# A one-core macaron block: pieces of the first stage split and moved, scales by a TensorE sum, attention's first group begun with its values

## The chip, the cores and the metric

One Trainium2 chip, one core of it. The metric is the time of one execution on the device in microseconds (us); for the kernel before it is the median of three runs.

## The reference, cut to what matters

x has 2 sequences of 2048 tokens of 1024 values. Three layers follow one another, each on a layer norm of x:

```python
x = x + 0.5 * ffn(layernorm(x))
x = x + attn(layernorm(x), w_attn, w_o)   # blocks of 128 tokens, each sees itself and the one before
x = x + 0.5 * ffn(layernorm(x))
# ffn(x): thought = layer_norm(x)[:, -1, :] @ agg_w + agg_b       (one row for each sequence)
#         4 times: thought += gelu(layer_norm(thought) @ d1_w + d1_b) @ d2_w + d2_b
#         gate = sigmoid(x @ gate_w + gate_b)
#         return layer_norm(x + gate * (thought @ bc_w + bc_b))
# attn:   weights = square(relu(masked q k^T)); out = (weights @ v) @ w_o^T, no softmax
```

All values are float32. The thought is a chain over one row for each sequence, with 4 x 2 large weight matrices of 16 MB; everything else works on 32 tiles of 128 tokens.

## The kernel before, in words

**One written plan.** `whole_plan` makes a list of pieces such as `("gate", n, h, third)` or `("norm", n)`. The programs of TensorE, ScalarE, DVE, GpSimd and SyncE (which issues all transfers) each walk the same list and issue their own part of every piece, in its order, with semaphore waits in front. An engine that waits holds up all that stands behind it in its own program, and nothing else. `paced(main, other, pace)` puts `pace` pieces of the second list behind each piece of the first that TensorE works on (`PE_PIECES`); `("rest",)` is an empty piece, for distance. `with_thought` spreads the steps of the thought chain (`t_...`) by an estimate of TensorE's time.

**Stages.** Stage 1 folds w_q and w_k into one matrix (`fold`, "qk"), then turns w_o and folds it with w_v ("vo"), and makes the gates of the 32 tiles (`gate`, two halves of three thirds of 8 matmuls each, 1.7 to 1.9 us a third). In this stage the thought of the first ffn runs beside them: its weights (512 KB a load) stream through a ring of slots, read from HBM twice or three times; in its first round ScalarE takes sums of their magnitudes (L1381), later it rounds them to a first float16 part and DVE makes the second (`t_high`, `t_low`, L1400 and L1754), which SyncE stores. Stage 2 is attention by groups of two tiles: q by 8 pieces, v, scores, collect; beside it the first ffn's end for the next group (`prep_...`). Stage 3 is the second ffn.

**Float16 pairs.** Weights and tokens are split in two float16 parts each, and a product is three float16 products. A weight matrix is scaled first by a power of two from its largest magnitude: `gate_max` or the fold's own maxima for each of 8 row blocks (L1463, L1470), `scale_a`, where DVE takes their maximum in each partition (L1475) and GpSimd the maximum over partitions (L1844), and `scale_b`, five small DVE steps. Then ScalarE rounds (`round`, L1266) and DVE takes the rest (`split`, L1496).

**A gate tile.** SyncE fetches x (`x`, L873) into a ring of 3; DVE takes moments and GpSimd the reciprocal root (L1423 to L1433, L1818, L1825); ScalarE applies the norm in the same piece (`norm`, L1282); TensorE turns the tile into two turn banks (`turn`, L1032; w_o goes through the same two banks, `wo_turn`), ScalarE and DVE empty them (L1236, L1274, L1440). The product goes to one of 4 product banks; DVE scales it and adds the bias (L1448), ScalarE takes the sigmoid in the same piece (L1295) and `gate_store` writes it (L877). The split gate weights are themselves written to HBM for stage 3 (`gate_save`, L882), eight transfers of 512 KB during the fold "vo", with the loads of gamma and beta (`params`, L884) behind them.

**The fold.** A finished row block is copied by ScalarE (L1252) into one of 2 slots, whose maximum DVE takes (L1470) and which SyncE stores (`fold_store`, L852); a copy waits until the store of the block two before has landed. The stored blocks come back later by `fold_rows` (L865).

**Attention's first group.** q needs the turned pairs of both of its tiles (`group_turn`, a transposing transfer, L944), v of a tile only that tile's. `plan_products` puts all of q first.

## Time and profile before

| | us |
|---|---|
| median of 3 runs | 2115.19 (2111.64 to 2117.34) |
| the profiled execution, its own time | 2117.86 |
| its span | 2116.6 |
| TensorE busy | 2037.7 (96%) |
| DVE busy | 1173.0 (55%) |
| ScalarE busy | 664.7 (31%) |
| GpSimd busy | 159.0 (8%) |
| mean transfer rate | 263 GB/s |

The profiler took one execution. Busy time is that of instructions; a matmul's end is modelled, so busy TensorE need not be at its peak. In timelines each line is the start, the time taken (both us), the engine, the line of the kernel, the operation and its tiles, the count, and in brackets the idle time before it with what ended it. PE is TensorE, ACT ScalarE, POOL GpSimd, SPq SyncE's queue of issues.

### The profile page before, as it was taken

The page shows a single profiled execution, that of the slowest core. Times are in us where ns is not written, and L with a number is a line of the kernel's source. Part 1 is how long each engine was busy: PE and PEld are TensorE (multiplying, and loading weights), DVE is VectorE, ACT ScalarE, POOL GpSimd, SP SyncE. Part 2 cuts the span into 40 slices and gives each one's busy share as a digit, 9 for nine tenths or more (in the row PEclk, how much of TensorE's full clock was granted, in tenths as well). Part 3 has the DMA queues.
Part 4 walks back from the last instruction along what each step waited for, and adds up shares of the span by engine and source line. Part 5 has one row for each costly group of instructions (what it writes and reads, how often), then busy time and mean ns, then how long its engine had stood idle before and what let it go on. Part 6 is the DMA issues. An engine that isn't in the chain of part 4 may idle for free.

```text
span 2116.6 us, 30247 instructions
## 1 busy us (share of the span) xinstructions
PE 2037.7 (96%) x11872; PEld 1037.0 (49%) x11872; DVE 1173.0 (55%) x2108; ACT 664.7 (31%) x931; POOL 159.0 (8%) x281
## 2 busy tenths in 40 slices
PE   8988989999999999998999999999999999999997
PEld 3333433444333446655665555665556564444443
DVE  2321323554344465567676755655555545888887
ACT  0557322433223232222333221211212113444443
POOL 0000000000000010000000000000000000111111
PEclk9999999999999999999999999999999999999999
DMA  8788897988988833348989799898987947555552
GB/s 340 237 311 341 285 353 269 379 319 320 354 338 333 332 132 118 100 140 299 323 294 327 273 320 293 297 347 283 313 290 278 357 149 221 149 151 154 154 149 80
DMA packets 275213, 555.76 MB, mean 263 GB/s; under 512 B 149040, under 2 KB 149248, under 8 KB 274688
## 3 DMA queue, kind: packets, MB, share of 16 engines
q1 hardware_dynamic: 275072, 553.83, 75.5%
q8 instruction: 95, 1.56, 0.3%
q14 instruction: 46, 0.38, 0.0%
HBM read 406.93 MB, written 113.26 MB: 246 GB/s over the span
## 4 chain that ended last, share of the span: by engine, by line
PE 47%; DMA 3%; DVE 2%; SPq 2%; ACT 1%; issue 1%; POOL 0%; ACTq 0%; DVEq 0%
PE product_banks L1023 41%; PE product_banks L1143 3%; PE thought_acc L1208 3%; DMA thought_units<-parts_scratch 1%; DMA gate_arena<-arena 1%; DMA arena<-in_x 0%; SPq L810 0%; DVE thought_units L1754 0%; SPq L944 0%; DMA thought_units<-in_d_w 0%; ACT arena L1315 0%; PE thought_turn L1216 0%; ACT arena L1318 0%; PE thought_acc L1198 0%; DVE arena L1566 0%
## 5 line engine op out<-in xcount | busy, mean ns | idle before, releaser
L1023 PE MATMUL product_banks<-gate_arena,arena 128*128 128x512 f16 x1536 | 354.1, 382 | 0.0
L1023 PE MATMUL product_banks<-wide_a,thought_units 128*128 128x512 f16 x1536 | 331.7, 379 | 0.0
L1023 PE MATMUL product_banks<-gate_arena,wide_a 128*128 128x256 f16 x2688 | 307.5, 274 | 2.4 <-DMA gate_arena<-arena 2.4
L1023 PE MATMUL product_banks<-wide_b,gate_arena 128*128 128x512 f16 x1344 | 301.8, 380 | 0.0
L1023 PEld LDWEIGHTS product_banks<-gate_arena,wide_a 128*128 128x128 f16 x2688 | 260.4, 98 | 59.5 <-issue 28.9
L1054 PE MATMUL product_banks<-wide_a,wide_b 128*128 128x512 f32 x512 | 240.9, 616 | 7.1 <-DMA wide_a<-in_w_attn 6.3
L1023 PEld LDWEIGHTS product_banks<-gate_arena,arena 128*128 128x128 f16 x1536 | 145.0, 98 | 203.6 <-issue 51.0
L1023 PEld LDWEIGHTS product_banks<-wide_a,thought_units 128*128 128x128 f16 x1536 | 150.3, 98 | 181.6 <-DVE arena L1606 0.5
L1023 PEld LDWEIGHTS product_banks<-wide_b,gate_arena 128*128 128x128 f16 x1344 | 127.2, 98 | 167.5 <-issue 24.9
L1423 DVE BATCH_NORM_STATS2 bn_parts<-arena 128x6 f32<-128x512 f32 x256 | 164.3, 684 | 4.4
L1054 PEld LDWEIGHTS product_banks<-wide_a,wide_b 128*128 128x128 f32 x512 | 95.1, 195 | 137.9 <-issue 137.8
L1448 DVE SCALAR_TENSOR_TENSOR arena<-product_banks,inverse_gate,arena 128x512 f32<-128x512 f32 x64 | 47.9, 750 | 176.5 <-PE product_banks L1023 175.6
L1818 POOL TENSOR_TENSOR token_stats<-stats,minus_half 128x1 f32<-128x1 f32 x96 | 61.3, 639 | 1083.4 <-DVE stats L1431 909.5
L1575 DVE SCALAR_TENSOR_TENSOR gate_arena<-product_banks,gate_arena 128x256 f16<-128x256 f32 x128 | 54.1, 423 | 152.5 <-ACT gate_arena L1330 150.2
L1336 ACT ACTIVATE arena<-product_banks,inverse_vo 128x512 f32<-128x512 f32 x64 | 44.0, 687 | 243.1 <-PE product_banks L1023 243.1
L1208 PE MATMUL thought_acc<-thought_units,thought_parts 128*6 128x512 f16 x1328 | 101.6, 383 | 19.1 <-DMA thought_units<-parts_scratch 10.2
L1143 PE MATMUL product_banks<-arena,key_weights 128*128 128x512 f32 x248 | 112.9, 600 | 6.1 <-issue 3.2
L1818 POOL TENSOR_TENSOR stats<-stats,minus_half 128x1 f32<-128x1 f32 x64 | 65.2, 1019 | 703.6 <-DVE stats L1431 419.3
L1330 ACT ACTIVATE gate_arena<-product_banks 128x256 f16<-128x256 f32 x128 | 41.4, 379 | 222.9 <-PE product_banks L1023 222.9
L1307 ACT ACTIVATE arena<-arena,token_stats 128x1024 f32<-128x1024 f32 x32 | 39.5, 1235 | 226.6 <-DMA arena<-in_x 226.6
L1364 ACT ACTIVATE arena<-arena 128x512 f32<-128x512 f32 x64 | 40.3, 630 | 175.2 <-DVE arena L1448 175.2
L1566 DVE SCALAR_TENSOR_TENSOR arena<-arena 128x1024 f16<-128x1024 f32 x32 | 39.2, 1225 | 97.2 <-ACT arena L1318 97.1
(168 smaller groups left out, 2090.1 us busy)
## 6 DMA issues: line engine op xcount, KB each, us to landing
thought_units<-parts_scratch SPq DMA_DIRECT2D x268, 512.0 KB, 6.1
thought_units<-in_d_w SPq DMA_DIRECT2D x148, 512.0 KB, 6.7
thought_row<-in_d_w SPq DMA_DIRECT2D x76, 512.0 KB, 7.2
arena<-in_x SPq DMA_DIRECT2D x64, 512.0 KB, 8.8
parts_scratch<-thought_units SPq DMA_DIRECT2D x64, 512.0 KB, 6.2
x_scratch<-arena SPq DMA_DIRECT2D x64, 512.0 KB, 6.8
arena<-x_scratch SPq DMA_DIRECT2D x40, 512.0 KB, 6.0
gate_scratch<-arena SPq DMA_DIRECT2D x32, 512.0 KB, 8.3
```

The lines of the kernel that those rows point to most:

```text
L1023: mm = pe.matmul(bank, left(i, k), right(j, k), start=(n == 0), stop=(n == 3 * KD - 1))
L1054: mm = pe.matmul(bank_ap(key), wide_b[:, e, d * P:(d + 1) * P], wide_a[:, e, h * BANK:(h + 1) * BANK], start=(e == 0), stop=(e == KD - 1))
L1143: mm = pe.matmul(bank_ap(key), weights_of(u)[:, side, :], value_slot(other)[:, h * BANK:(h + 1) * BANK], start=(side == 0), stop=(side == ...
L1208: mm = pe.matmul(thought_acc[at:at + PARTS * B, :], value, unit[:, part, h * BANK:(h + 1) * BANK], start=first and part == 0, stop=last an ...
L1307: act.activation(ph_slots[u % PREP_RING], px_slots[u % PREP_RING], ACT.Identity, bias=st[:, 1:2], scale=st[:, 0:1]).then_inc(h0_made, 1)
L1330: act.activation(queries[:, query_place(n * GROUP + i), 0, e - 1:e + 1, :], made[:, i], ACT.Copy, scale=QUERY_SCALE).then_inc(q_high_made, 1)
L1336: act.activation(value_slot(n * GROUP + i)[:, h * BANK:(h + 1) * BANK], bank_ap(key), ACT.Copy, scale=inverse["vo"][:, :]).then_inc(out_of ...
L1364: act.activation(res, res, ACT.Sigmoid).then_inc(gated_3, 1)
L1423: dve.bn_stats(bn_parts[:, h, :], source[:, h * BANK:(h + 1) * BANK]).then_inc(own.up(), 1)
L1448: dve.scalar_tensor_tensor(out=res[:, cols], in0=bank_ap(key), scalar=inverse["gate"][:, :], in1=bias[:, cols], op0=ALU.mult, op1=ALU.add) ...
L1575: low = dve.scalar_tensor_tensor(out=q[:, 1], in0=made[:, i], scalar=QUERY_SCALE, in1=q[:, 0], op0=ALU.mult, op1=ALU.subtract)
L1818: return pool.tensor_tensor(to, st[:, 2:3], minus_half[:, 0:1], ALU.pow)
```

## The change

In stage 1 the sigmoid becomes a piece of its own: that of a tile's first half after the first third of the second half, that of the second half after the first third of the next tile. ScalarE's part of a norm becomes `norm_h`, after the second third of a gate tile (and, for tiles 0 and 1, earlier in the first fold, with DVE's part of norm 1 moved ahead of the turns of tile 0). The pace of the pieces beside the first fold goes from 0.8 to 0.9. For scales DVE's maximum is `scale_t`; in `scale_a` TensorE multiplies it by a matrix filled with 1/1024, which gives every partition the sum over partitions, and DVE scales it back; GpSimd's reduction goes. The scale so comes from a sum of 128 maxima instead of the largest. `scale_a` takes a turn bank. `gate_save` and `params` move from the fold "vo" to the gate tiles behind it, among the row fetches and splits, whose pace goes from 0.3 to 0.6 of a list that is longer by them. In group 0 of attention the six thirds of v of tile 0 come ahead of q. SyncE's, TensorE's and DVE's waits follow the new places.

```diff
@@ -365,8 +365,14 @@
             out.append(("gate", n, h, third))
-            if n and (h, third) == (1, 0):
-                out.append(("gate_store", n - 1))
+            if n and (h, third) == (0, 0):
+                out.append(("sigmoid", n - 1, 1))
+            if (h, third) == (0, 1) and n + 2 < TILES:
+                out.append(("norm_h", n + 2))
+            if (h, third) == (1, 0):
+                out.append(("sigmoid", n, 0))
+                if n:
+                    out.append(("gate_store", n - 1))
     return out
@@ -440,6 +446,10 @@
             products = products[:-PARTS]
+        if n == 0:
+            own = [p for p in products if p[0] == "v" and p[2] == 0]
+            products = own + [p for p in products if p not in own]
         if more:
@@ -489,12 +499,12 @@
     gate_rows += [("gate_max", k) for k in range(KD)]
-    gate_rows += [("scale_a", "gate"), ("rest",), ("rest",), ("scale_b", "gate")]
+    gate_rows += [("scale_t", "gate"), ("rest",), ("scale_a", "gate"), ("rest",), ("scale_b", "gate")]
     gate_rows += rounded_ahead("gate", [])
...
     gate_rows += [("x", 1), ("x", 2)] + [("wo_rows", n) for n in range(wo_ahead)] + [("norm", 0), ("rest",)]
-    gate_rows += [("rest",), ("rest",), ("turn", 0, 0), ("turn", 0, 1), ("norm", 1)]
-    fold_qk = paced(plan_fold("qk"), gate_rows, 0.8, PE_PIECES)
+    gate_rows += [("norm_h", 0), ("norm", 1), ("rest",), ("norm_h", 1), ("turn", 0, 0), ("turn", 0, 1)]
+    fold_qk = paced(plan_fold("qk"), gate_rows, 0.9, PE_PIECES)
     fold_qk.append(("fold_store", "qk", KD - 1))
@@ -502,15 +512,17 @@
     early = paced([p for n in range(EARLY) for p in plan_gate(n)], wo, 0.9, PE_PIECES)
-    save = [("gate_save", k) for k in range(KD)] + [("params",)] + [("rest",)] * 6 + [("half_params",)]
-    fold_vo = paced(plan_fold("vo"), save, 0.5, PE_PIECES)
-    fold_vo.append(("fold_store", "vo", KD - 1))
+    fold_vo = plan_fold("vo") + [("fold_store", "vo", KD - 1)]
     splits = []
     for m in ("qk", "vo"):
-        splits += [("fold_rows", m, 0), ("fold_rows", m, 1), ("scale_a", m), ("rest",), ("scale_b", m)]
+        splits += [("fold_rows", m, 0), ("fold_rows", m, 1), ("scale_t", m), ("rest",), ("scale_a", m), ("rest",), ("scale_b", m)]
         splits += rounded_ahead(m, [("fold_rows", m, k) for k in range(2, KD)])
+    save = [("params",)] + [("rest",)] * 5 + [("half_params",)]
+    for k in range(KD):
+        save += [("gate_save", k)] + [("rest",)] * 3
+    splits = paced(splits, save, 0.75)
     splits += [("prep_fetch", 0), ("rest",), ("rest",), ("prep_norm", 0), ("prep_beta", 0)]
-    gates = paced([p for n in range(EARLY, TILES - LATE) for p in plan_gate(n)], splits, 0.3, PE_PIECES)
+    gates = paced([p for n in range(EARLY, TILES - LATE) for p in plan_gate(n)], splits, 0.6, PE_PIECES)
     out = [("start",)]
@@ -518,7 +530,7 @@
     out += paced([p for n in range(TILES - LATE, TILES) for p in plan_gate(n)], prep, 1.15, PE_PIECES)
-    out.append(("gate_store", TILES - 1))
+    out += [("sigmoid", TILES - 1, 1), ("gate_store", TILES - 1)]
     out.append(("score_scale",))
@@ -553,12 +565,16 @@
 TURN_AT = {piece: n for n, piece in enumerate(
-    p for p in PLAN if p[0] in ("turn", "wo_turn"))}
+    p for p in PLAN if p[0] in ("turn", "wo_turn", "scale_a"))}
 SPLIT_TURN_AT = {piece: n for n, piece in enumerate(
...
+SCALE_AT = {piece[1]: n for n, piece in enumerate(p for p in PLAN if p[0] == "scale_b")}
@@ -1055,6 +1071,14 @@
                         mm.then_inc(product_full, 1)
+            elif kind == "scale_a":
+                m, = a
+                at = TURN_AT[(kind, m)]
+                if at >= TURN_BANKS:
+                    pe.wait_ge(turn_out[at % TURN_BANKS], at // TURN_BANKS)
+                pe.wait_ge(top_found, SCALE_AT[m] + 1)
+                pe.matmul(turn_ap((kind, m))[:, 0:1], mean_maker[:, :], scale_stat[m][:, KD:KD + 1], start=True,
+                          stop=True).then_inc(turn_full, 1)
             elif kind == "wo_turn":
@@ -1088,8 +1112,6 @@
                         pe.wait_ge(group_in[i], 16 * (n + 1))
-                    if n == 0:
-                        pe.wait_ge(split_done, split_total("vo"))
                 group, cols = group_of(n), slice(e * P, (e + 1) * P)
@@ -1103,6 +1125,9 @@
                     await_free(pe, key)
+                    if n == i == h == 0:
+                        pe.wait_ge(group_in[0], 16)
+                        pe.wait_ge(split_done, split_total("vo"))
                 group, cols = group_of(n), slice(h * BANK, (h + 1) * BANK)
@@ -1259,7 +1284,7 @@
                 if k == 0:
-                    act.wait_ge(scale_made, ("gate", "qk", "vo").index(m) + 1)
+                    act.wait_ge(scale_made, SCALE_AT[m] + 1)
                     if m != "gate":
@@ -1274,10 +1299,10 @@
                     turn_out[at % TURN_BANKS], 1)
-            elif kind == "norm":
+            elif kind == "norm_h":
                 n, = a
                 xt, st = x_slots[n % X_RING], token_stats[:, TILE_OF[n], :]
-                act.wait_ge(rstd_made, MOMENT_AT[(kind, n)] + 1)
+                act.wait_ge(rstd_made, MOMENT_AT[("norm", n)] + 1)
                 act.wait_ge(x_in[n % X_RING], 16 * (n // X_RING + 1))
@@ -1288,8 +1313,8 @@
                 round_half((kind, n, h), as_pair(pair_slots[n % PAIR_RING])[:, 0])
-            elif kind == "gate" and a[2] == 2:
-                n, h, _ = a
+            elif kind == "sigmoid":
+                n, h = a
                 await_out(act, ("gate", n, h))
@@ -1471,15 +1496,20 @@
+                at = TURN_AT[(kind, m)]
+                dve.wait_ge(turn_full, at + 1)
+                dve.tensor_scalar(scale_stat[m][:, KD:KD + 1], turn_ap((kind, m))[:, 0:1], float(D), TINY, ALU.mult,
+                                  ALU.max).then_inc(turn_out[at % TURN_BANKS], 1)
+            elif kind == "scale_t":
+                m, = a
                 dve.wait_ge(largest[m], KD)
...
                 top, exponent, scale = (scale_stat[m][:, KD + i:KD + i + 1] for i in range(3))
-                dve.wait_ge(top_shared, ("gate", "qk", "vo").index(m) + 1)
-                dve.tensor_scalar(top, exponent, TINY, None, ALU.max).then_inc(own.up(), 1)
-                dve.wait_ge(own.sem, own.n)
+                await_turned(dve, ("scale_a", m))
                 dve.tensor_scalar(exponent.bitcast(I32), top.bitcast(I32), EXPONENT_BITS, None,
@@ -1838,11 +1868,6 @@
                 pool.wait_ge(zeroed, 1)
-            elif kind == "scale_a":
-                m, = a
-                pool.wait_ge(top_found, ("gate", "qk", "vo").index(m) + 1)
-                pool.partition_all_reduce(scale_stat[m][:, KD + 1:KD + 2], scale_stat[m][:, KD:KD + 1], P,
-                                          bass.bass_isa.ReduceOp.max).then_inc(top_shared, 1)
             elif kind == "norm":
```

## Rows read from the trace of the kernel before

**Rows 1.** The page, part 1: busy us, share of the span, instructions.
```profile
PE 2037.7 (96%) x11872; PEld 1037.0 (49%) x11872; DVE 1173.0 (55%) x2108; ACT 664.7 (31%) x931; POOL 159.0 (8%) x281
```

**Rows 2.** Stretches: length, busy PE, PEld, DVE, ACT, POOL, then PEclk, DMA share, GB/s.
```profile
150.10:229.10 79.00, 61.24 (x351) 27.36 (x351) 19.48 (x49) 53.66 (x94) 2.92 (x8) 0.93 0.88 331
229.10:370.00 140.90, 134.56 (x425) 52.12 (x426) 45.53 (x61) 36.33 (x42) 0.71 (x1) 0.96 0.84 297
370.00:730.00 360.00, 349.64 (x2038) 143.70 (x2037) 157.35 (x341) 118.93 (x158) 24.86 (x52) 1.00 0.90 346
...
784.60:812.40 27.80, 23.73 (x194) 20.13 (x194) 11.90 (x20) 3.84 (x8) 0.55 (x1) 0.88 0.39 135
```

**Rows 3.** Timeline, ScalarE and TensorE, 153 to 180 us.
```profile
153.81 1.24 ACT L1282 ACTIVATE arena<-arena,token_stats 128x1024 f32<-128x1024 f32 x1 [1.84 <-POOL token_stats L1825]
155.10 1.97 PE L1032 MATMUL turn_banks<-identity,arena 128*128 128x128 f32 x8 [5.01 <-ACT arena L1282]
156.86 3.15 PE L1023 MATMUL product_banks<-gate_arena,arena 128*128 128x512 f16 x8
...
161.41 1.89 PE L1023 MATMUL product_banks<-gate_arena,arena 128*128 128x512 f16 x8
...
178.07 1.09 PE L1032 MATMUL turn_banks<-identity,arena 128*128 128x128 f32 x8
```

**Rows 4.** Waits of TensorE for transfers, 156.5 to 229.2 us: total, times, longest.
```profile
PE thought_acc L1198 <- DMA thought_units<-in_d_w: 3.3, 4, 1.6
PE turn_banks L1032 <- DMA arena<-in_w_o: 3.0, 1, 3.0
PE thought_acc L1198 <- DMA thought_row<-in_d_w: 2.7, 2, 1.8
```

**Rows 5.** Waits of ScalarE, 156.5 to 229.2 us: total, times, longest.
```profile
ACT arena L1282 <- POOL token_stats L1825: 10.5, 3, 3.6
ACT arena L1295 <- DVE arena L1448: 6.9, 2, 4.1
```

**Rows 6.** Timeline, 257 to 301 us: TensorE, SyncE's store of the fold, ScalarE.
```profile
257.76 0.60 PE L1208 MATMUL thought_acc<-thought_units,thought_parts 128*6 128x512 f16 x8
258.30 3.70 PE L1054 MATMUL product_banks<-wide_a,wide_b 128*128 128x512 f32 x8
...
279.38 1.17 SPq L852 DMA_DIRECT2D vo_scratch<-arena  x2
...
288.48 1.07 ACT L1252 COPY arena<-product_banks 128x512 f32<-128x512 f32 x2 [11.39 <-DMA vo_scratch<-arena]
...
293.92 1.02 PE L1208 MATMUL thought_acc<-thought_units,thought_parts 128*6 128x512 f16 x8 [6.34 <-DVE t_wide L1761]
294.87 5.91 PE L1054 MATMUL product_banks<-wide_a,wide_b 128*128 128x512 f32 x8
```

**Rows 7.** Stores of the gates' weights (landing; issue ns), and one stretch of 10 us.
```profile
gate_pair_scratch<-gate_arena SPq DMA_DIRECT2D x8, 512.0 KB, 8.2
...
L882 SPq DMA_DIRECT2D gate_pair_scratch<-gate_arena x8: 478/844/1638, 233.5 to 282.2; - x8
...
280.00:290.00 10.00, 7.57 (x24) 2.96 (x16) 0.35 (x1) 1.52 (x3) 0.00 (x0) 1.00 1.02 419
```

**Rows 8.** Timeline where attention begins, and 48 like matmuls later.
```profile
784.72 1.63 SPq L944 DMA_TRANSPOSE thought_units<-arena  x1
...
788.69 23.83 PE L1023 MATMUL product_banks<-thought_units,wide_a 128*128 128x256 f16 x192 [4.07 <-DMA thought_units<-arena]
...
1033.70 5.41 PE L1023 MATMUL product_banks<-gate_arena,wide_a 128*128 128x256 f16 x48
```

**Rows 9.** Timeline, GpSimd's reduction for the scale of qk.
```profile
399.90 0.38 POOL L1844 PARTITION_ALL_REDUCE scale_stat_qk<-scale_stat_qk  x1 [6.71 <-issue]
```

**Rows 10.** Gate rows' issues and landing (us), DVE's thought norm, TensorE behind it.
```profile
22.84 10.20 SPq L836 DMA_DIRECT2D arena<-in_gate_w  x8
...
DMA to landing us min/median/max: 14.9/15.3/15.8
...
42.06 0.50 DVE L1696 TENSOR_SCALAR thought<-centred,t_small 128x8 f32<-128x8 f32 x2 [0.90 <-POOL t_small L1861]
...
43.00 0.29 PE L1178 MATMUL thought_turn<-thought,mean_maker 128*128 128x16 f32 x2
```

**Rows 11.** SyncE's own waits, 0 to 800 us: at `gate_store`.
```profile
SPq L877 <- ACT arena L1295: 17.0, 5, 10.5
```

More of the change, by code:

```diff
@@ L620, in macaron_kernel @@
     d1_bias = sbuf("d1_bias", [P, KH])
-    scale_stat = {m: sbuf(f"scale_stat_{m}", [P, KD + 3]) for m in ("gate", "qk", "vo")}
-    inverse = {m: sbuf(f"inverse_{m}", [P, 1]) for m in ("gate", "qk", "vo")}
+    scale_stat = {m: sbuf(f"scale_stat_{m}", [P, KD + 3]) for m in SCALE_AT}
+    inverse = {m: sbuf(f"inverse_{m}", [P, 1]) for m in SCALE_AT}
     score_scale = sbuf("score_scale", [P, 1])
@@ L717, in macaron_kernel @@
     largest = {m: sem(f"largest_{m}") for m in ("gate", "qk", "vo")}
-    top_found, top_shared = sem("top_found"), sem("top_shared")
+    top_found = sem("top_found")
     high_made, split_done = sem("high_made"), sem("split_done")
@@ L1502, in vector_program @@
             elif kind == "score_scale":
-                dve.wait_ge(scale_made, 3)
+                dve.wait_ge(scale_made, len(SCALE_AT))
                 dve.tensor_scalar(score_scale[:, :], inverse["qk"][:, :], 1.0 / (QUERY_SCALE * TOKEN_SCALE * P),
```

## The prediction, made before the change was run

> **What bounds the kernel now.** I read the page first, then a table of stretches, then the waits of TensorE, then the timeline around its longest waits. TensorE is busy in 2037.7 of 2116.6 us [rows 1]: only about 79 us can be won without taking matmuls away. The stretches show where the edit's share of them lies [rows 2]: 17.8 us idle in 150.1 to 229.1 (early gate tiles and the turning of w_o), 6.3 us in 229.1 to 370 (the second fold), 10.4 us in 370 to 730 (gate tiles with weights split), and 4.1 us in 784.6 to 812.4, where attention begins. So four places count, and each has another cause.
>
> First, 5.01 us before 155.10 [rows 3]: TensorE wants to turn tile 1, whose norm ScalarE ends only then, because DVE's moments came late. Second, the remaining 12.7 us up to 229.1: 9.0 us on transfers [rows 4] and 3.7 us, by subtraction, on ScalarE and DVE emptying turn banks. ScalarE is there stopped at the head of its queue, 10.5 us for GpSimd's reciprocal root and 6.9 us for DVE in front of a sigmoid [rows 5], with bank copies and weight maxima (which SyncE's fetches wait for) behind it. Third, 6.34 us before 293.92: ScalarE cannot copy a finished product of the fold, since the slot's store was issued at 279.38 and freed ScalarE only at 288.48; DVE's copy of the sums, which TensorE wants, is queued behind that [rows 6]. Stores of the gates' weights lie among those transfers and take 8.2 us to land [rows 7]. Fourth, 4.07 us before 788.69, the turned copy of the second token tile, issued at 784.72 [rows 8].
>
> Each of these waits is followed by matmuls at a lower granted clock: the stretch 784.6 to 812.4 has a mean of 0.88, between the levels 1.2 and 2.4 GHz [rows 2], and the same eight operations take longer right after a wait [rows 3, 6].
>
> **The change part by part.**
>
> *Norms apart, tile 1 early.* DVE's and GpSimd's part of norm 1 now stands some six fold pieces before turn 1, ScalarE's part (`norm_h`) in between. The wait of 5.01 us goes. With it goes the slow clock: eight turns in 1.97 instead of 1.09 us, eight matmuls in 3.15 instead of 1.89 us [rows 3]. Together 5.01 + 0.88 + 1.26 = 7.2 us. In later tiles `norm_h` comes after two thirds of a gate product, and still four thirds, some 7 us, before the turn that needs it; one norm takes 1.24 us [rows 3], so nobody waits for it.
>
> *Norms and sigmoids, to 229.1.* No instruction is added; those behind them on ScalarE come earlier. Of the 3.7 us on banks I take half, 1.8. Of the 9.0 us on transfers, 3.0 is a row of w_o whose fetch SyncE issues behind fetches that wait for ScalarE; I take half, 1.5. The rest stays, and grows: the stretch moved 331 GB/s for 79 us [rows 2], 26.1 MB, and 10 us at a full share moved 419 GB/s [rows 7], so it can't be shorter than 62.4 us. TensorE without waits would need about 79 - 17.8 - 2.1 = 59. What is won at 155 thus meets transfers that are nearly full; I give 2.0 us back. Net 1.3 us won; bounds: 8 won (the stretch near its 62.4, beyond the 7.2) and 5 lost. The lower clock after the last turns I leave as it is.
>
> *Sigmoids and the queue of SyncE.* The sigmoid of a tile's second half moves behind the next tile's first third, `gate_store` stays. Between them are three thirds, some 5 us, for one short operation. SyncE already waits for sigmoids there, 17.0 us in 5 waits [rows 11], and the fetches behind it wait with it. I cost it at nothing, for the three thirds cover it; without that cover it is the slower rival.
>
> *Gates' weights stored later.* Eight stores of 0.52 MB, issued from 233.5 to 282.2, and two parameter loads leave the second fold; at 419 GB/s each holds the transfer engines 1.25 us, so the eight hold them 10 us, and SyncE for some 0.5 to 1.6 us each [rows 7]. Without them the fetches on which SyncE's earlier steps wait land sooner, and so the fold's store is both issued and landed some us earlier. TensorE stood from 293.92 - 6.34 = 287.6 on, so all of the wait goes if ScalarE's 288.48 comes forward by 6.3 us, and part of it with less. The wait is worth 6.34 + (1.02 - 0.60) + (5.91 - 3.70) = 9.0 us, taking the slow rows against the same forms at full clock [rows 6]; I take 8, as this wait has two causes and both shrink. Bounds: 2 (only the issue order changes) and 9. The parameters are first read long after, by `half_params`, which moves with them.
>
> *The same stores in the gate stretch.* It has 10.4 us of idle TensorE at a transfer share of 0.90, 346 GB/s [rows 2]. The ten transfers add 12.5 us of transfer time to 36 us of room; the rows to be split also come some 20% denser, as 200 pieces shrink to about 165. Where the share is full, a store pushes every fetch behind it back by 1.25 us. I take 3.5 us lost; bounds 0 and 8.
>
> By a page of the Trainium skill, DMA: Bandwidth & Descriptors, section Where 436 GB/s comes from, about 358 GB/s on the HBM side bind such transfers. By it the 124.6 MB of this stretch and 5.2 MB more would need 362.5 us, more than the stretch now lasts, so every added store would cost its full time there. The trace speaks against it, with 419 GB/s over 10 us.
>
> *Scales from a sum by TensorE.* DVE's steps stay as many. Three partition reductions leave GpSimd (0.38 us each, with 6.71 us idle before the second) [rows 9]; no engine was held up by them while TensorE ran, so 0 won. TensorE gains three tiny matmuls, under 0.3 us each by its nearest row [rows 10]: 0.4. It also waits now for DVE's maximum, two plan pieces behind; behind a late maximum all of TensorE would stand. For qk and vo DVE has pieces to spare. For the gates, the maxima of the rows move forward: one more stands in front of DVE's `t_var`, and the first now stands ahead of the fold's own two maxima. The rows land 14.9 us after issue at 22.84, so the first near 37.7 and the second near 39; DVE's step that ended at 42.56 moves back by about one maximum of 1.2 us and the wait for the first row, 1.5 to 2 us, and TensorE's 43.00 has 0.4 us of room [rows 10]. 1.5 us lost, bounds 0 and 3.
>
> *Attention begins with values.* v of tile 0 needs only the first turned copy, so 6 thirds, some 10 us, cover the second. Won: 4.07 and the slow clock, 23.83 us for 192 matmuls against 4 x 5.41 [rows 8] = 2.2; 6.3 us. Late next: the first scores have 3 instead of 9 thirds between them and the last queries, some 5 us in which DVE must finish the last pair of queries behind the tokens it prepares; I expect no wait. Bounds 2 and 6.5.
>
> **Sum.** -7.2 - 1.3 - 8.0 + 3.5 + 0.4 + 1.5 - 6.3 = -17.4 us. The profiled execution took 2117.86 us (span 2116.6, 1.3 around it), 2.7 above the median of 2115.19. 2117.9 - 17.4 = 2100.5 on its own scale, 2115.2 - 17.4 = **2098 us** for a median. Stages after this one only shift.
>
> **The rivals.**
> - *Transfers are the bound* (0.20). The 155 to 229 stretch gives 2 us in all, the fold 6, the gate stretch takes 8, the start of attention gives 6, scales take 2: -4, **2111 us**. For: shares of 0.88 and 0.90 [rows 2]. Against: a tenth of the transfer time is still unused. The page above would have it so.
> - *The fold's wait stays* (0.13): the store is late since SyncE waits for splits of thought weights, not since the bus is full. Then 8 becomes 1, -10.4: **2105 us**. For: SyncE's queue waits for ScalarE and DVE at every such split. Against: that chain itself waits for fetches slowed by the stores.
> - *More comes back* (0.12): the stretch to 229 reaches its bound of 8 instead of 1.3, since ScalarE's 17.4 us of waits [rows 5] were behind most of what TensorE waits for, and the gate stretch takes nothing: -17.4 - 6.7 - 3.5 = -27.6, **2088 us**.
> - *SyncE waits for late sigmoids* (0.06), slower: in each of 25 middle tiles it stands at `gate_store` for a sigmoid now behind turns, and thought fetches behind it come later. It decides once the wait exceeds what the ring of fetched weights covers; at 1 us each 25 us are lost, -17.4 + 25 = +7.6, **2123 us**. Against: 5 waits in 32 stores now.
> - That the edit does not do what it says has no room here: the order of instructions is written out. Little net effect by a mixture of mishaps: 0.04.
>
> **How the numbers follow.** My forecast has 0.45 and spans 2092 to 2104. The range over cases reaches from 2087 to 2111, leaving out half of the best case, part of the transfer case and the slower ones. A measurement of this kernel can tell about 0.3%, 6.3 us, from no change: faster means under 2108.8. Faster: 0.45 + 0.13 + 0.12 and a half of 0.20, 0.80. Same 0.14, slower 0.06.
>
> **What would show it.** Right: no TensorE wait of 5 us near 150 and none near 287, the q product without a wait, stores of the gates' weights spread over 380 to 650, granted clock 1.0 in the 10 us after 150 and after 287. Wrong: idle TensorE in 370 to 730 over 20 us; a wait of ScalarE on the fold's store still near 11 us; SyncE's waits at `gate_store` summing to over 40 us; a new wait before the first scores. I'd be wrong altogether if the time around 229 came out where it is now.

## The result, and the profile after

2105.35 us median against 2114.78 for the kernel before, 11 runs each: ratio 0.996, 95% interval 0.9943 to 0.9976. It is 0.4% faster, 8.5 us by the ratio and 9.4 by the medians, about half of what was forecast. The median lies outside 2092 to 2104, the span given to the forecast alone, and inside 2087 to 2111, the range over all cases. The profiled execution took 2104.01 us, span 2102.8. The page and the same stretches as in [rows 1, 2]:

```profile
PE 2035.0 (97%) x11878; PEld 1034.0 (49%) x11878; DVE 1172.2 (56%) x2108; ACT 664.0 (32%) x931; POOL 161.1 (8%) x278
```

```profile
150.10:229.10 79.00, 72.06 (x387) 29.98 (x386) 20.39 (x46) 56.06 (x97) 2.18 (x6) 0.96 0.90 350
229.10:370.00 140.90, 138.05 (x488) 53.30 (x488) 49.52 (x69) 42.35 (x49) 1.43 (x3) 0.99 0.81 292
370.00:730.00 360.00, 344.35 (x1997) 141.36 (x1995) 155.80 (x344) 113.62 (x151) 27.20 (x50) 0.99 0.90 346
784.60:812.40 27.80, 27.80 (x225) 21.85 (x224) 16.13 (x25) 8.45 (x14) 1.26 (x3) 1.00 0.36 123
```

TensorE's idle time fell from 17.8 to 6.9, from 6.3 to 2.9 and from 4.1 to 0 us in three stretches, and rose from 10.4 to 15.7 in the gate stretch. Fixed windows cut the work at different places in two kernels, so everything below goes by the work: the start of the same matmul in each timeline, in one profiled execution of each kernel. Matmuls 128 to 192 of the first fold take 39.4 in both and are left out. Numbers in us:

| from, to | before | after | difference | forecast |
|---|---|---|---|---|
| span's start, first matmul | 5.9 | 5.5 | -0.4 | |
| first fold, matmuls 0 to 128 | 65.1 | 66.6 | +1.5 | +1.5, gate maxima |
| first fold, 192 to 224 | 22.3 | 24.3 | +2.0 | |
| from there to the second fold | 96.4 | 87.5 | -8.9 | -8.5, tile 1 and the freer ScalarE |
| the second fold | 143.1 | 135.9 | -7.1 | -8.0 |
| gate tiles 3 to 27 | 368.3 | 375.2 | +6.9 | +3.9 |
| gate tile 28 to attention's first collect | 97.9 | 91.6 | -6.3 | -6.3 |
| the rest | 1278.3 | 1276.8 | -1.5 | |

The sum is -13.8, that of the two spans. ScalarE's waits for GpSimd and DVE in 156.5 to 229.2 [rows 5] are gone, and TensorE's for transfers are 5.8 instead of 9.0 [rows 4]. These are ScalarE's three longest there, then TensorE's:

```profile
ACT wide_a L1299 <- PE turn_banks L1048: 11.9, 8, 3.2
ACT thought_units L1406 <- DMA thought_row<-in_d_w: 2.4, 3, 1.7
ACT thought_units L1406 <- DMA thought_units<-in_d_w: 1.4, 2, 1.2
...
PE thought_acc L1223 <- DMA thought_units<-in_d_w: 2.9, 2, 2.1
PE thought_acc L1223 <- DMA thought_row<-in_d_w: 2.9, 1, 2.9
```

The timeline of after, at the places of [rows 10, 3, 6, 8] in turn, with the one new wait of 2 us ahead of the second fold, at 134.79:

```profile
43.20 0.49 DVE L1726 TENSOR_SCALAR thought<-centred,t_small 128x8 f32<-128x8 f32 x2 [0.90 <-POOL t_small L1886]
43.76 0.40 PE L1203 MATMUL thought_turn<-thought,mean_maker 128*128 128x16 f32 x2 [0.88 <-DVE thought L1726]
...
134.79 1.04 PE L1223 MATMUL thought_acc<-thought_units,narrow_in 128*6 128x512 f32 x8 [2.04 <-DMA thought_units<-in_d_w]
...
154.85 1.09 PE L1048 MATMUL turn_banks<-identity,arena 128*128 128x128 f32 x8
155.78 1.89 PE L1039 MATMUL product_banks<-gate_arena,arena 128*128 128x512 f16 x8
...
269.77 1.26 SPq L868 DMA_DIRECT2D vo_scratch<-arena  x2
276.51 1.07 ACT L1277 COPY arena<-product_banks 128x512 f32<-128x512 f32 x2 [8.99 <-DMA vo_scratch<-arena]
281.95 0.60 PE L1233 MATMUL thought_acc<-thought_units,thought_parts 128*6 128x512 f16 x8 [2.85 <-DVE t_wide L1791]
...
778.28 10.52 PE L1039 MATMUL product_banks<-wide_b,thought_units 128*128 128x512 f16 x48
788.64 21.12 PE L1039 MATMUL product_banks<-thought_units,wide_a 128*128 128x256 f16 x192
...
825.99 0.67 PE L1168 MATMUL product_banks<-arena,key_weights 128*128 128x512 f32 x1 [1.91 <-DVE key_weights L1623]
```

TensorE turns tile 1 with no wait and at full clock (1.09 us instead of 1.97). Behind the wait at 134.79 the granted clock was 0.83 on average from 136 to 146, and what that costs falls into the fourth difference of the table, not into the third. ScalarE still waits 8.99 us for the fold's store, and TensorE 2.85 of the 6.34 us. Attention begins without a wait, and the queries take 21.12 instead of 23.83 us; the first collect waits 1.91 us, where it had waited 1.08 in before.

In the gate stretch a new wait stands at 676.69, among the four fetches of attention's first group, which now stand 20 of TensorE's pieces earlier; and SyncE's waits at `gate_store` are twice those of [rows 11]:

```profile
662.33 0.36 SPq L943 DMA_DIRECT2D arena<-in_x  x1
662.73 0.43 SPq L947 DMA_DIRECT2D arena<-gate_scratch  x1
...
676.69 1.89 PE L1223 MATMUL thought_acc<-thought_units,narrow_hidden 128*6 128x512 f32 x8 [3.32 <-DMA thought_units<-in_d_w]
678.51 3.60 PE L1039 MATMUL product_banks<-gate_arena,arena 128*128 128x512 f16 x8
```

```profile
SPq L893 <- ACT arena L1320: 34.1, 9, 10.2
```

A second new wait, 2.71 us at 632.45, is no wait of TensorE for a transfer, but one begins its chain. A row of the fold is fetched at 621.09 and frees ScalarE only at 628.85; the copy of a turn bank stands behind that on ScalarE, DVE's part of the bank behind the copy, and DVE's copy of the sums, which TensorE wants, behind that:

```profile
621.09 0.43 SPq L881 DMA_DIRECT2D arena<-vo_scratch  x1
628.85 1.15 ACT L1291 ACTIVATE wide_b<-arena,scale_stat_vo 128x1024 f16<-128x1024 f32 x1 [9.93 <-DMA arena<-vo_scratch]
630.51 1.29 DVE L1465 SCALAR_TENSOR_TENSOR arena<-turn_banks,arena 128x512 f16<-128x512 f32 x2 [5.43 <-ACT arena L1261]
631.72 0.68 DVE L1791 COPY t_wide<-thought_acc 128x512 f32<-128x512 f32 x1
632.45 0.66 PE L1241 MATMUL thought_turn<-identity,t_wide 128*128 128x128 f32 x4 [2.71 <-DVE t_wide L1791]
```

### The profile page after: what moved, and what is told of

Same layout as the page of the kernel before. It is cut to its first block and busy times, and to the rows that moved or that the text cites. A ratio compares the mean times of both kernels' runs of the same rounds, so it can differ in the third digit from the quotient of the medians.

```text
span 2102.8 us, 30246 instructions
## 1 busy us (share of the span) xinstructions
PE 2035.0 (97%) x11878; PEld 1034.0 (49%) x11878; DVE 1172.2 (56%) x2108; ACT 664.0 (32%) x931; POOL 161.1 (8%) x278
```

## The experiments

Twelve kernels, each an edit of the changed kernel unless it says otherwise. Ratios are against runs of the kernel before on the same chip; the stretches are those of the table above, from the one profiled execution.

| | ratio, 95% interval | second fold begins | fold | gates 3 to 27 | 28 to collect |
|---|---|---|---|---|---|
| before | 1 | 229.0 | 143.1 | 368.3 | 97.9 |
| after | 0.996, 0.9943 to 0.9976 | 223.3 | 135.9 | 375.2 | 91.6 |
| e1 saves back in the fold | 0.9981, 0.9967 to 0.9996 | 220.7 | 139.5 | 374.6 | 91.6 |
| e2 pace 0.52 for 0.6 | 0.9981, 0.9966 to 0.9996 | 226.5 | 136.7 | 378.0 | 91.6 |
| e3 saves in the last tiles | 0.993, 0.9909 to 0.9952 | 219.9 | 137.0 | 366.3 | 91.6 |
| e4 saves twice | 0.9997, 0.9978 to 1.0015 | 220.3 | 136.5 | 382.7 | 91.6 |
| e5 ScalarE's order as before | 1.0017, 1.0 to 1.0034 | 229.1 | 139.1 | 380.0 | 91.7 |
| e6 queries first | 0.9973, 0.996 to 0.9987 | 219.6 | 135.8 | 375.4 | 95.8 |
| e7 = e3, maximum on GpSimd | 0.9928, 0.9906 to 0.9951 | 222.0 | 134.9 | 368.5 | 91.6 |
| e8 = e7, gate maxima later | 0.9928, 0.9903 to 0.9953 | 221.7 | 138.3 | 371.4 | 91.6 |
| e9 = e3, four fold slots | 0.9904, 0.988 to 0.9929 | 223.1 | 131.3 | 369.3 | 91.6 |
| e10 group fetches later | 0.9933, 0.9906 to 0.9959 | 223.1 | 138.6 | 370.4 | 91.6 |
| e11 = before, saves in last tiles | 1.0018, 1.0002 to 1.0034 | 229.6 | 139.7 | 371.7 | 97.6 |
| e12 = e9 + e8 | 0.9911, 0.9884 to 0.9938 | 223.2 | 131.3 | 371.1 | 91.6 |

Some of these share their plan up to a point and so show the scatter of one execution: the second fold begins at 219.6 to 226.5 in after, e2, e4, e6 and e10, which are the same up to there; the fold takes 135.8 to 138.6 in the same five. A difference below 3 us of one stretch is thus no finding by itself. The stretch from matmul 224 to the second fold scatters more, 84.3 to 90.0 in eight kernels with the same plan there (mean 86.5; before 96.4, e11 97.3), and so does the rest behind the first collect, 1275.2 to 1281.2. The intervals of e1, e2, e3, e6, e7, e8 and e10 overlap that of after; of the edits of the changed kernel only e4 and e5 (slower) and e9 and e12 (faster) are clear of it by time alone.

**e1, saves back in the fold.**

```diff
-    fold_vo = plan_fold("vo") + [("fold_store", "vo", KD - 1)]
+    save = [("gate_save", k) for k in range(KD)] + [("params",)] + [("rest",)] * 6 + [("half_params",)]
+    fold_vo = paced(plan_fold("vo"), save, 0.5, PE_PIECES)
+    fold_vo.append(("fold_store", "vo", KD - 1))
...
-    splits = paced(splits, save, 0.75)
...
-    gates = paced([...], splits, 0.6, PE_PIECES)
+    gates = paced([...], splits, 0.32, PE_PIECES)
```

> The changed kernel, but the eight stores of the gates' weights and the parameter loads are back in the second fold and the splits of qk and vo are paced as before. Stretches of TensorE, in us, before / changed: second fold (its first matmul to gate tile 3) 143.1 / 135.9; gate tiles 3 to 27: 368.3 / 375.2. Theory: the stores made the fold's own store late, and the same stores with the denser row fetches cost the gate tiles 7: fold 141 to 144, gate tiles 367 to 370, total as the changed kernel within 3 us. Rival: the relief of ScalarE won the fold's stretch: it stays at 135 to 137, and the total falls by 7 against the changed kernel.

The fold's wait came back, but both stretches missed the theory (139.5 for 141 to 144, 374.6 for 367 to 370), and the rival too. The gates did not get shorter, for a wait of another kind came:

```profile
283.14 1.02 PE L1231 MATMUL thought_acc<-thought_units,thought_parts 128*6 128x512 f16 x8 [6.62 <-DVE t_wide L1789]
...
392.11 1.11 PE L1046 MATMUL turn_banks<-identity,arena 128*128 128x128 f32 x4 [4.96 <-DVE scale_stat_qk L1500]
```

The stores make 3.6 us of the fold (139.5 against 135.9), not 8.

**e2, a slower pace** of the list beside the gates (0.52 for 0.6).

> The changed kernel with the list of splits and stores paced at 0.52 instead of 0.6, so that the first fetch for the tiles' preparation (4 transfers) falls at piece 343 of the plan instead of 318 (before: 338). Theory: those four transfers among the thought's weight fetches made the wait of 3.3 us near 677 and the slow clock behind it: gate tiles 3 to 27 take 371 to 372 instead of 375.2, the fold stays at 136. Rival: the eight stores themselves are the price: 374 to 376.

The gates took 378.0, more than theory or rival had. What made them longer also shows what the second wait of e1 is. DVE (first three rows) and TensorE (last two):

```profile
394.29 1.29 DVE L1784 SCALAR_TENSOR_TENSOR thought_units<-thought_row,unit_scale,thought_units 128x1024 f16<-128x1024 f32 x1 [4.04 <-ACT thought_units L1425]
396.80 1.28 DVE L1784 SCALAR_TENSOR_TENSOR thought_units<-thought_row,unit_scale,thought_units 128x1024 f16<-128x1024 f32 x1 [1.23 <-ACT thought_units L1425]
398.00 0.15 DVE L1502 TENSOR_SCALAR scale_stat_qk<-turn_banks 128x1 f32<-128x1 f32 x1
...
389.29 0.28 PE L1080 MATMUL turn_banks<-scale_stat_qk,mean_maker 128*128 128x1 f32 x2
398.21 1.11 PE L1048 MATMUL turn_banks<-identity,arena 128*128 128x128 f32 x4 [8.14 <-DVE scale_stat_qk L1502]
```

TensorE's sum for the scale sits in one of the two turn banks. The 0.15 us step of DVE that empties it is queued behind two splits of thought weights, which wait for ScalarE. So the next tile's turn waits 8.14 us. In after this cost nothing, by the luck of its pace. The wait of 676.69 was not there, but one of 2.49 us stood at 704.32, ahead of the group's fetches, which here come at 722. The wait of 2.7 us for the fold's row was not there either.

**e3 and e4, the stores of the gates' weights moved away, and doubled.** e3 drops them from the gate stretch (pace 0.355) and puts them into the last four gate tiles; e4 stores each block a second time, into a second tensor:

```diff
+    late = [p for n in range(TILES - LATE, TILES) for p in plan_gate(n)]
+    late = paced(late, [("gate_save", k) for k in range(KD)], 0.5, PE_PIECES)
+    out += paced(late, prep, 1.15, PE_PIECES)
```

> The changed kernel with the eight stores in the last four gate tiles, where the share of the transfer engines was 0.3, and the splits paced as before. Theory: gate tiles 3 to 27 take 367 to 370 as before the change, the fold stays at 135 to 137, the last tiles and the start of attention lose under 1; in all 5 to 8 us less than the changed kernel, 15 less than before. Rival: the gate tiles' loss comes from the sigmoids and norms that stand later on ScalarE: they stay at 374 to 376 and nothing is won.

> The changed kernel with each of the eight stores issued twice, the second time to a scratch tensor that nobody reads: 4.2 MB more in the gate tiles. Theory of a full transfer queue: each store costs up to 1.25 us where the share is full, so the gate tiles take 380 to 385 instead of 375.2. Rival: only a few ill-placed transfers cost, and there is room for the others: 375 to 378.

e3 takes 8.9 us from the gates and gives none back in the last tiles, which have room. It moves more than the stores, for with its pace the group's fetches come at 696 instead of 663 us. Eight more stores cost 7.6 us, 0.95 us each. The stretch of e4 moved 351 GB/s, that of after 347:

```profile
356.81:739.55 382.74, 362.56 (x2081) 149.18 (x2078) 163.68 (x358) 120.51 (x160) 27.92 (x52) 0.98 0.91 351
```

The Trainium skill, DMA: Bandwidth & Descriptors, section Where 436 GB/s comes from, puts the limit on the HBM side at about 358 GB/s; an estimate from that figure is 1.5 us for each store of 524 KB, if the stretch were full. The trace does not bear that out: 0.95 us of time for each, at 351 GB/s.

**e5, ScalarE's norm and sigmoid in their old pieces**, norm 1 still early.

```diff
-            elif kind == "norm_h":
+            elif kind == "norm":
...
-            elif kind == "sigmoid":
-                n, h = a
+            elif kind == "gate" and a[2] == 2:
+                n, h, _ = a
```

> The changed kernel, but ScalarE's part of a norm stands in the same piece as DVE's and GpSimd's again, and the sigmoid in the last third of its half, as before the change. Norm 1 stays ahead of the first turns. Theory (ScalarE standing at the head of its queue for GpSimd's root and DVE's bias add is what makes TensorE wait for turn banks and rows between 155 and 229): its waits of about 10 and 7 us come back, the start of the second fold moves from 223.3 to 226 to 228, and the stretch of the fold after it stays at 135 to 137. Rival 1 (only the early norm 1 counted): 223.3 within 1 us, total within 2 us of the changed kernel. Rival 2 (SyncE's long waits in gate_store, 34 us against 17 before, cost the later gate tiles something): gates 3 to 27 become 2 to 4 us shorter than 375.2.

ScalarE's two waits came back in size, and gate tile 0 began at 152.3, 4.6 us ahead of before; at the second fold all of that was gone, 229.1:

```profile
ACT arena L1307 <- POOL token_stats L1855: 10.6, 3, 3.6
...
ACT arena L1320 <- DVE arena L1473: 7.6, 3, 3.9
```

```profile
PE thought_acc L1223 <- DMA thought_units<-in_d_w: 6.5, 3, 3.2
PE turn_banks L1048 <- DMA arena<-in_w_o: 4.5, 1, 4.5
PE turn_banks L1048 <- ACT wide_a L1299: 2.4, 2, 1.2
```

(TensorE's waits, 150 to 235.) The second fold began later than the theory's 226 to 228. The whole is 0.0057 of the ratio, 12 us, the dearest part of the change that a run took out; norm and sigmoid went back together, and no run parts them. The gates were 4.8 us longer too, though SyncE waited only 17.7 us at `gate_store`: no cost of those waits shows.

**e6, queries first** in group 0, as before.

> The changed kernel, but in attention's first group all of the queries come ahead of the values again. Theory: from gate tile 28 to the first collect it takes 97 to 98.5 us instead of 91.6, nothing earlier moves by over 1 us beyond scatter, and the total is 6 us longer (ratio about 0.999 against the kernel before). Rival (the 4 us wait comes from transfers that the new gate stretch places differently): no wait before the first query, 93 us or less.

```profile
778.46 22.39 PE L1039 MATMUL product_banks<-thought_units,wide_a 128*128 128x256 f16 x192 [3.54 <-DMA thought_units<-arena]
```

4.2 us came back, not 6: a wait of 3.5 instead of 4.1 us, the queries 22.39 us instead of 23.83, and the first collect's wait 0.8 us shorter than in after (826.62 less the end of the work ahead of it, 820.19 + 5.34, is 1.1).

**e7 and e8, the maximum over partitions back on GpSimd** (from e3), and in e8 one more empty piece ahead of the gate maxima. The rest of the edit takes out `scale_t` and TensorE's and DVE's parts of `scale_a`.

```diff
+            elif kind == "scale_a":
+                m, = a
+                pool.wait_ge(top_found, SCALE_AT[m] + 1)
+                pool.partition_all_reduce(scale_stat[m][:, KD + 1:KD + 2], scale_stat[m][:, KD:KD + 1], P,
+                                          bass.bass_isa.ReduceOp.max).then_inc(top_shared, 1)
```

> As the version with the saves of the gates' weights in the last four gate tiles (span 2095.3, ratio 0.993), but the maximum over partitions goes back to GpSimd, so that it takes no turn bank and no matmul. Theory (TensorE's wait of 3.0 us in the turn behind the scale of qk is there because DVE empties the scale's bank only behind splits that wait for ScalarE and a transfer): that wait goes, gates 3 to 27 take 362 to 364 instead of 366.3, span about 2092, ratio 0.991 to 0.992. Rival (the wait moves to the next thing that DVE has late): 366 within 1 us. Rival (GpSimd's 6.7 us before its reduction now holds up the reciprocal roots behind it): over 367.

> As the one before, with one empty piece more ahead of the maxima of the gate rows, so that these stand where they stood before the change. Theory: TensorE's wait of 0.9 us near 43.8 goes, block 128 of the first fold begins near 71.0 instead of 72.1, and the total is 1 us shorter, which lies under what the timing tells apart. Rival: the gates' first rounding comes late instead and a wait shows up behind 54: block 128 at 72 or later.

The 3.0 us wait of e3 went, another of 3.9 us came (3.8 in e8), the gates took 368.5 as the second rival had it, and the ratio did not move. The new wait is GpSimd's. In e7:

```profile
559.05 0.38 POOL L1861 PARTITION_ALL_REDUCE scale_stat_vo<-scale_stat_vo  x1 [7.91 <-issue]
560.58 0.17 DVE L1709 TENSOR_SCALAR t_small<-t_small 128x2 f32<-128x2 f32 x1
566.10 0.73 POOL L1878 TENSOR_TENSOR t_small<-t_small,minus_half 128x2 f32<-128x2 f32 x1 [6.67 <-issue]
566.87 0.23 DVE L1716 SCALAR_TENSOR_TENSOR centred<-centred,t_small,vectors 128x8 f32<-128x8 f32 x1 [6.11 <-POOL t_small L1878]
571.57 1.02 PE L1225 MATMUL thought_acc<-thought_units,thought_parts 128*6 128x512 f16 x8 [3.91 <-DVE thought_parts L1764]
```

DVE's input for the reciprocal root is there at 560.75; GpSimd, which has just made the reduction, starts on it only at 566.10. In e8 the first fold's block at matmul 128 began at 71.0 (e7 71.8), as the theory had it, and no median can tell that. The wait of 0.9 us near 43.8 is in nine of the ten kernels with the maxima moved forward, and in none of before, e8, e11 and e12.

**e9, four slots for the second fold's blocks** (from e3); two of them are row slots, empty by then.

```diff
-    fold_slots = [tile_at(8 + i) for i in range(FOLD_RING)]
+    fold_slots = [tile_at(8 + i) for i in range(2 * FOLD_RING)]
+    slots_of = {"qk": FOLD_RING, "vo": 2 * FOLD_RING}
...
+                if m == "qk" and k in (1, 2):
+                    sp.wait_ge(fold_out[FOLD_RING + k - 1], 16 * 2)
+                    sp.wait_ge(largest["vo"], KD - 2 + k)
```

> As the version with the saves of the gates' weights in the last four gate tiles, but the second fold has four slots for finished row blocks instead of two (it borrows two of the row slots, empty by then), so that ScalarE copies a block without waiting for the store of the block two before. Theory (what is left of TensorE's wait in the second fold is that store's landing, 6.7 us, issued late): ScalarE's wait of 8.8 us for it goes, TensorE's 3.05 us near 281 goes with the slow clock behind it, the fold stretch takes 133 to 134 us instead of 137.0, ratio 0.991 to 0.992. Rival (the thought chain behind ScalarE is late by its own fetches, the slot only happens to end last): 136 to 137.5, another wait of 2 to 3 us in the same place.

The whole wait went. The fold's stretch, and ScalarE's copies in it, now released by TensorE:

```profile
223.08:354.41 131.33, 131.33 (x442) 51.27 (x443) 45.28 (x60) 37.80 (x44) 0.70 (x1) 1.00 0.79 286
```

```profile
270.06 0.58 ACT L1286 COPY arena<-product_banks 128x512 f32<-128x512 f32 x1 [3.02 <-PE product_banks L1075]
```

TensorE is busy all the time and at full clock in it; no wait is left there to win. Ratio 0.9904, 2096.56 us median: the lowest ratio of all, with its runs within 2.7 us of each other. Four slots were not tried with the stores in the fold.

**e10, the fetches of attention's first group later**, where they stood before.

```diff
+    splits += [("rest",)] * 12
     splits += [("prep_fetch", 0), ("rest",), ("rest",), ("prep_norm", 0), ("prep_beta", 0)]
```

> The changed kernel with twelve empty pieces ahead of the fetches of attention's first group, which so stand at TensorE's piece 338, as before the change, instead of 318. Theory (these four fetches collide with fetches for the thought at 662 to 676 us): TensorE's wait of 3.3 us at 676.7 and the slow clock behind it go, gates 3 to 27 take 369 to 371 us instead of 375.2, the total is 4 to 6 us shorter, ratio 0.993 to 0.994. Rival (the stores of the gates' weights make the late thought fetches late): the wait is there again within 1 us of its size, 374 to 376. Second rival (it moves to where the fetches now are, near 700): the same sum.

The wait near 676 is not there. The matmuls of the thought at the same place:

```profile
675.45 1.04 PE L1224 MATMUL thought_acc<-thought_units,narrow_hidden 128*6 128x512 f32 x8
```

The stretch is 370.4 us, as the theory had it. In e4, e5 and e6, which leave the fetches where after has them, the wait is there again, 3.2 to 3.8 us. The intervals of e10 and after against before overlap, and the profiled span of e10 is 1.7 us longer than that of after, since other stretches scattered the other way; so the 4.8 us rest on this one stretch and this wait.

**e11, the kernel before with its saves in the last gate tiles** and nothing else.

> The kernel before, with one part of the change alone and put elsewhere: the eight saves of the gates' weights and the two parameter loads leave the second fold, the saves go to the last four gate tiles. Theory (the fold gains by their leaving, and the late gate tiles have room for them): the fold stretch 137 to 139 us instead of 143.1, gates 3 to 27 at 368 within 2 us, up to 229 nothing moves, total 5 to 7 us shorter, ratio 0.997. Rival (without the earlier tile 1 and the free ScalarE the fold's wait stays): 142 or more, ratio 0.999 or more.

Neither theory nor rival held: the fold got 3.4 us shorter, the gates 3.4 longer, and the whole none (1.0018). Its wait in the fold is still 4.28 us:

```profile
292.08 0.73 PE L1209 MATMUL thought_acc<-thought_units,thought_parts 128*6 128x512 f16 x8 [4.28 <-DVE t_wide L1762]
```

**e12, e9 and e8 together.**

> The version with four slots and late saves (span 2093.8, ratio 0.9904), with the maximum over partitions back on GpSimd and the maxima of the gate rows where they stood before the change. Theory (the 3.7 us before 399.96, DVE emptying the scale's turn bank late, is worth its size and the 6.8 us of half clock around it): block 128 of the first fold begins at 71.0, the fold stretch stays at 131 to 132, gates 3 to 27 take 363 to 366 us instead of 369.3, span about 2088, ratio 0.988 to 0.989. Rival (as in the version with late saves, where the same edit took the wait away and others of the same size came): gates 368 to 370, ratio 0.990 to 0.992.

The rival held, but for the gates, 371.1 instead of 368 to 370. The wait at 400 us went, GpSimd's at 569.5 was 5.19 us, and the ratio stayed (0.9911 against 0.9904).

## Why the prediction came out as it did

*Tile 1 and the freer ScalarE* (-8.5 forecast, -8.9 measured). The sum held (-9.9 by the mean of the eight kernels, so that the fit to 0.4 is luck), the split between the two terms did not. I gave 7.2 us to tile 1 and 1.3 to norms and sigmoids. By e5 tile 1 alone keeps 1.2 us of this stretch, less than the scatter: its gain of 4.6 us is handed back before the second fold, as TensorE runs into a ScalarE that is still stopped at the head of its queue and into rows of w_o fetched late behind it. The relief of ScalarE is what lets the gain through, and it works in the later tiles too, where I had costed it at nothing. What that relief would do without the early norm 1 was not run.

*The fold* (-8.0, -7.1). By the step "all of the wait goes if ScalarE's 288.48 comes forward by 6.3": reckoned from the fold's start, the copy's release did come forward, from 59.4 to 53.2 us (288.48 - 229.04, 276.51 - 223.28), 6.2 us. But TensorE got there 2.7 us sooner as well, since the slow clock that followed the last turns, which I had left as it was, had gone. The first 10 us of the fold, before and then after, with a clock of 0.73 and 1.00:

```profile
229.04:239.04 10.00, 10.00 (x19) 4.52 (x20) 2.51 (x3) 3.09 (x3) 0.00 (x0) 0.73 0.72 238
```

```profile
223.28:233.28 10.00, 10.00 (x25) 4.67 (x26) 4.15 (x12) 3.08 (x3) 0.70 (x1) 1.00 0.63 218
```

6.34 - 6.2 + 2.7 is the 2.85 us that still stand. The gain was so 2.7 of clock and 4.4 of wait, with the slow clock behind the wait in it. And the stores were only half of its cause: 3.6 us by e1, 3.4 by e11. The store itself landed in 6.7 us (269.77 to 276.51) instead of 9.1; e9, where the wait for a slot is gone and TensorE's with it, shows that two slots were too few even with the stores away. The rival "the fold's wait stays" was half true.

*The gate stretch* (+3.9 forecast, +6.9 measured). This is the term that failed, though it stayed inside its bounds. I priced the ten transfers and left the rest of the list's shift at nothing. By e10, 4.8 us of it are the group's fetches, moved 20 pieces forward with the denser list, among fetches of thought weights for which TensorE then waits; by the doubling in e4 the stores themselves are some 7.6. e3 took both away, and 8.9 us with them, while a bank wait of 3.0 came: 11.9, near 7.6 + 4.8. Against that stand 4.8 us that the freer ScalarE gives by e5. 7.6 + 4.8 - 4.8 is near the 6.9 measured, but each is of one profiled execution, and the sum closing so well is partly luck. Read from the waits, 5.3 of the 6.9 us are idle time (15.7 against 10.4); the longest wait is the 3.32 us of the group's fetches, and the next the 2.71 us in which ScalarE stands at the head of its queue for a row of the fold. I had not thought of that one. It is there in all five kernels with the stores among the gates at a pace of 0.6 (2.7 to 4.2 us) and not in e2 at 0.52, so the pace is the likelier cause; no run was made for it.

*Scales* (+0.4, no engine held up by GpSimd). Wrong twice, though the total did not show it: the turn bank that the sum occupies can stop TensorE for 3.0 to 8.1 us (e1, e2, e3), and GpSimd's reduction, which I held free, stops it 3.8 to 5.2 us where the thought's reciprocal root comes right behind it (e7, e8, e12). In before the next input for GpSimd came 12 us later. *Gate maxima* (+1.5, +1.5) came as worked out, and not by one execution alone: matmuls 0 to 128 take 66.4 us on average in the ten kernels with the maxima moved forward, 65.0 in the four without. The *start of attention* (-6.3, -6.3) did too; e6 gives 4.2 of it back. Within it two small errors cancel: the slow clock was worth 2.7 us (23.83 against 21.12) and not 2.2, and "I expect no wait" before the first scores left out 0.8 us at the first collect, which comes sooner behind its values.

*The forecast as a number.* Its terms came to -17.4, the profiles to -13.8, the medians to -9.4. The step from -13.8 to -9.4 is scatter and none of the change: the profiled execution of before lay 3.1 us above its median (2117.86, 2114.78), that of after 1.3 below. I had noted 2.7 of it and then took the whole sum, read from that execution, off the median. That the median of 2105 is the very number of the rival "the fold's wait stays" is chance: by that rival the fold would have given 1 us, and it gave 7.1. Of the signs of being right, one came by halves, for near 287 a wait of 2.85 us is left at 281.95; of the signs of being wrong none came (15.7 us idle in 370 to 730, ScalarE's wait 8.99, SyncE's 34.1).

*SyncE's waits at `gate_store`* doubled, and no run shows a cost of theirs; the rival that built on them took them for a cause. *Transfers as the bound*: a store more costs 0.95 us in the gate stretch, none in the last tiles. They bound by place more than by rate: e10 moved 352 GB/s in its gate stretch, after 347, and e10 was the shorter by 4.8 us.

What stays open: why e11's gate stretch rose by 3.4 us, though no store and only the two parameter loads were added to it (TensorE is idle for 14.0 us there against 10.4, and its two longest waits, 2.71 us at 515.4 and 1.94 at 411.0, are for DVE and ScalarE and for no transfer), and the stretch of the first fold around 134.8, longer than in before by 0.5 us in e5 and by 0.7 to 2.9 in all the others that share the change's early pieces; no run was made for it.

## What to carry to other kernels

An engine that serves two others should not stand at the head of its in-order queue for a third: split the step that waits off and put it where its input is surely there. Here that was worth 12 us, more than the longest wait of TensorE with the slow clock behind it (9.0), and one such place that is left, ScalarE waiting for a row of the fold, costs 2.7 us. Where a wait ends with a transfer out of a ring of two, count the slots before you thin the traffic. And when a paced list gets longer or denser, cost everything that slides with it, and every bank a new small product borrows: who empties it, and what stands ahead in that engine's queue.

## What the runs showed of the hardware

GpSimd pays for its reduction across partitions on both sides: the reduction itself shows as 0.38 us, but in e7 it is preceded by 7.9 us idle (of which 4.6 after its input was ready, 554.47), and the next small operation by 6.67 us, 5.4 of them with its input ready; in e8 and e12 that second gap is 6.63 and 7.03 us. It costs only where the input is there earlier: the first reduction of e7, for the gates, starts 0.14 us after its input, having stood idle for 7.4, and the operation behind it 0.09 us after its own, 19 us later. How much of the gaps is the reduction's own work cannot be told, as the profile's spans on GpSimd are rough. The Trainium skill, GPSIMD Engine Reference, section 2.1 Instruction dispatch, tells of some 6 us of code loading at the first call of a freshly loaded kernel; the gaps here are of that size, but they come again at the third call of the same program and on the way back too, and no run shows that code is loaded in them.

Waits of nearly one length can differ in what the slow clock behind them costs. The stretch of the first queries, in before and in e6:

```profile
788.69:812.00 23.31, 23.31 (x189) 19.74 (x190) 10.63 (x16) 3.21 (x7) 0.55 (x1) 0.88 0.32 119
```

```profile
778.46:802.00 23.54, 23.54 (x199) 19.98 (x200) 12.20 (x21) 3.76 (x9) 0.79 (x2) 0.94 0.40 141
```

Behind a wait of 4.07 us the mean clock was 0.88 and the 192 matmuls took 2.7 us more than at full clock; behind one of 3.54 us, 0.94 and 1.3. The length of the wait does not decide it alone: in the 10 us behind them the granted clock was 0.72 in before and 0.87 in e6, but behind a wait of 4.08 us in the fold of e5 it was 0.83.
